# A gated delta-rule layer with a ternary feed-forward: softmax and key scales of the projection cut into five pieces, and two scale vectors loaded in another stage

## What is computed

```python
q, k, v = (silu(causal_conv4(x @ W.T)) for W in (Wq, Wk, Wv))     # 4 heads of 64
beta    = sigmoid(x @ Wb.T)
delta   = chunked delta rule over 32 tokens (l2norm(q), l2norm(k), v*beta)
probs   = softmax((x @ gate_w + gate_b) / exp(log_temp), over 5)
probs   = probs * (1 - 5*eps) + eps
o       = probs[0..2] * (fir3(v), fir15(v), fir63(v)) + probs[3]*delta + probs[4]*v
x       = layernorm(x + rmsnorm(o) @ Wo.T)
```

## Time and profile before

| | us |
|---|---|
| median of 3 runs (2244.39 to 2247.52) | 2244.57 |
| the profiled execution's own time | 2240.09 |
| its span, first to last instruction | 2238.3 |
| PE busy in the span | 2050.4 (92%) |
| DVE / ACT / POOL busy | 1161.4 / 875.1 / 535.1 |

### The profile page before, as it was taken

One profiled execution on the slowest core, in us unless ns is written; L12 is line 12 of the kernel. 1 busy time (PEld: TensorE's weight loads), 2 busy tenths in 40 slices (PEclk: granted clock), 3 DMA queues, 4 the chain that ended last, 5 costly groups with the idle time before them and its releaser, 6 DMA issues.

```text
span 2238.3 us, 42120 instructions
## 1 busy us (share of the span) xinstructions
PE 2050.4 (92%) x17462; PEld 1741.1 (78%) x17462; DVE 1161.4 (52%) x1836; ACT 875.1 (39%) x1418; POOL 535.1 (24%) x628
## 2 busy tenths in 40 slices
PE   6887876875899999799999999999999999999998
PEld 5766665775888887588888888888888888888886
DVE  5878786885467676424434434433443443443442
ACT  4444443102344444334434433443443443443442
POOL 1237872885455555000000000000000000000000
PEclk9989997987799999899999999999999999999999
DMA  6655555987999996100000000000000000000000
GB/s 180 192 155 167 175 159 164 299 260 227 199 220 242 228 229 171 37 1 29 1 29 29 6 23 29 29 1 29 29 1 29 29 1 29 29 1 29 29 1 19
DMA packets 250623, 208.81 MB, mean 93 GB/s; under 512 B 159634, under 2 KB 215378, under 8 KB 247890
## 3 DMA queue, kind: packets, MB, share of 16 engines
q1 hardware_dynamic: 238162, 175.84, 29.0%
q10 hardware_dynamic: 12288, 30.41, 4.8%
HBM read 126.32 MB, written 75.76 MB: 90 GB/s over the span
## 4 chain that ended last, share of the span: by engine, by line
PE 57%; issue 1%; DVE 1%; ACT 1%; DMA 0%; ACTq 0%; POOLq 0%; DVEq 0%; SPq 0%; POOL 0%
PE B L1622 50%; PE O L1649 5%; PE T L1580 1%; DVE yb L1755 0%; ACT gate L1694 0%; DMA srow<-in_srow 0%; DVE stats L1817 0%; ACT L1694 0%; DVE z L1808 0%; DVE z L1812 0%; DVE xl L1735 0%; DVE z L1831 0%; POOLq L1522 0%; ACT xh L1682 0%; ACTq L1516 0%
## 5 line engine op out<-in xcount | busy, mean ns | idle before, releaser
L1708 ACT ACTIVATE yb<-B,scol 128x512 f32<-128x512 f32 x256 | 176.6, 690 | 580.3 <-PE B L1622 580.3
L1622 PE MATMUL B<-act1l,wr 128*128 128x512 f32 x1024 | 398.4, 389 | 0.0
L1622 PE MATMUL B<-act0h,wr 128*128 128x512 f32 x1024 | 398.3, 389 | 0.0
L1622 PE MATMUL B<-act0l,wr 128*128 128x512 f32 x1024 | 398.3, 389 | 0.0
L1622 PE MATMUL B<-act1h,wr 128*128 128x512 f32 x1024 | 398.3, 389 | 0.0
L1743 DVE TENSOR_TENSOR act0l<-yb,act0h 128x512 fp32r<-128x512 f32 x256 | 176.1, 688 | 317.3 <-ACT act0h L1711 315.1
L295 PE MATMUL proj<-xt,w_qkv 128*128 128x262 f32 x768 | 203.4, 414 | 74.8 <-DVE acc L466 61.6
L466 DVE SCALAR_TENSOR_TENSOR acc<-proj,taps,acc 128x512 f32<-128x512 f32 x288 | 213.9, 749 | 82.6 <-ACT acc L413 74.4
L1743 DVE TENSOR_TENSOR act1l<-yb,act1h 128x512 fp32r<-128x512 f32 x128 | 88.6, 692 | 295.5 <-ACT act1h L1711 295.5
L295 PEld LDWEIGHTS proj<-xt,w_qkv 128*128 128x128 f32 x768 | 147.5, 201 | 116.8 <-DVE acc L466 69.8
L1622 PEld LDWEIGHTS B<-act1l,wr 128*128 128x128 f32 x1024 | 192.2, 188 | 39.9
(11 more groups left out here) (177 smaller groups left out, 3174.3 us busy)
## 6 DMA issues: line engine op xcount, KB each, us to landing
qk_s<-yT SPq DMA_DIRECT2D x16, 1024.0 KB, 5.1
qk<-qk_s SPq DMA_DIRECT2D x32, 512.0 KB, 4.7
wraw<-in_ffn_w ACTq DMA_DIRECT2D x32, 352.0 KB, 4.9
toe<-in_toe_short ACTq DMA_DIRECT2D x32, 320.0 KB, 7.4
xt<-in_xt SPq DMA_DIRECT2D x16, 524.0 KB, 4.2
toe<-in_toe_long ACTq DMA_DIRECT2D x32, 256.0 KB, 6.0
kk_s<-kfull SPq DMA_DIRECT2D x16, 512.0 KB, 5.1
k_s<-ktok SPq DMA_DIRECT2D x16, 512.0 KB, 6.0
```

Source lines behind the costliest of these rows:

```text
L1622: last = nc.tensor.matmul(B[slot % 4][:, :], w, part, start=(k == 0 and i == 0), stop=(k == kts - 1 and i == len(parts) - 1))
L1708: last = nc.scalar.activation(dst, B[slot % 4][:, :], ACT.Gelu, scale=scol[:, slot:slot + 1])
```

## The change

In project the boundary work is cut into five pieces, put between the blocks of three steps t = 4c + 5, 4c + 6 and 4c + 7, which is 5, 6, 7 for part 0, 9, 10, 11 for part 1 and 13, 14, 15 for part 2: logits behind block 1 and maxima (with ssk0) behind block 2 of the first; key scales behind block 5 of the second; sums behind block 1 and shares behind block 2 of the third. Both exponentials go on ACT ahead of the tap of block 3 in the second step. The turning of the key scales and their copies move from the first to the third step, and POOL's substitution starts and ends one step later. The loads of `scol` and `srow` move from the head of ffn to the end of delta, behind those of `x1` and `xres`, with their tiles and their semaphore; the waits stay. The helpers `gate_logits` and `gate_shares` are cut in two, and part 3 calls them one after the other as before.

```diff
--- before.py
+++ after.py
-EARLY_COLS = {6: (0, 1, 8), 7: (0, 8, 14), 8: (0, 14, 20), 9: (0, 20, 31),
-              10: (1, 1, 8), 11: (1, 8, 14), 12: (1, 14, 20), 13: (1, 20, 27), 14: (1, 27, 31)}
+EARLY_COLS = {7: (0, 1, 8), 8: (0, 8, 14), 9: (0, 14, 20), 10: (0, 20, 31),
+              11: (1, 1, 8), 12: (1, 8, 14), 13: (1, 14, 20), 14: (1, 20, 26), 15: (1, 26, 31)}
...
-                    if c in range(EARLY) and t % PART_STEPS == 0:
+                    if c in range(EARLY) and t % PART_STEPS == 2:
...
+                def exponentials(t):
+
+                    c = t // PART_STEPS - 1
+                    if c in range(PARTS - 1) and t % PART_STEPS == 2:
+                        act.wait_ge(to_exp0, c + 1)
+                        if c < EARLY:
+                            act.wait_ge(small_out, (c + 1) * PART_STEPS + 1)
+                            if c:
+                                act.wait_ge(gam0_done, c)
+                            nc.scalar.activation(ebeta[:, :, :], raw[:, c * NE:c * NE + NE, NGATE:NGATE + HEADS], ACT.Exp,
+                                                 scale=-1.0).then_inc(exp0_done, 1)
+                        nc.scalar.activation(lg0[:, :, :, :], lg0[:, :, :, :], ACT.Exp).then_inc(exp0_done, 1)
...
                     for cb in range(CB):
+                        if cb == 3:
+                            exponentials(t)
...
                     step(t, t % 2, (t - 1) // 2, True, t < 2)
-                    if t % PART_STEPS == 0:
-                        c = t // PART_STEPS - 1
-                        act.wait_ge(small_out, t + 1)
-                        if c < EARLY:
-                            if c:
-                                act.wait_ge(gam0_done, c)
-                            nc.scalar.activation(ebeta[:, :, :], raw[:, c * NE:c * NE + NE, NGATE:NGATE + HEADS], ACT.Exp,
-                                                 scale=-1.0).then_inc(exp0_done, 1)
-                        act.wait_ge(to_exp0, c + 1)
-                        nc.scalar.activation(lg0[:, :, :, :], lg0[:, :, :, :], ACT.Exp).then_inc(exp0_done, 1)
...
-                    gate_logits(nc, link, keep, lg0, mx0, rows(c)).then_inc(to_exp0, 1)
-
-                def first_shares(c):
-                    dve.wait_ge(exp0_done, c + 1 + min(c + 1, EARLY))
-                    link(gate_shares(nc, link, keep, lg0, mx0, rows(c)))
+                    gate_logits(nc, link, keep, lg0, rows(c))
+
+                def first_maxima(c):
+                    gate_maxima(nc, link, lg0, mx0).then_inc(to_exp0, 1)
+                    if c < EARLY:
+                        dve.wait_ge(kk_summed, (c + 1) * PART_STEPS + 2)
+                        nc.vector.tensor_scalar(ssk0[:, :, :].rearrange("p (t b) h -> p t (b h)", b=BATCH),
+                                                kk[:, c * PART_STEPS:(c + 1) * PART_STEPS, :], L2_EPS, None, ALU.add)
 
                 def first_scales(c):
 
-                    dve.wait_ge(kk_summed, (c + 1) * PART_STEPS + 2)
-                    nc.vector.tensor_scalar(ssk0[:, :, :].rearrange("p (t b) h -> p t (b h)", b=BATCH),
-                                            kk[:, c * PART_STEPS:(c + 1) * PART_STEPS, :], L2_EPS, None, ALU.add)
                     dve.wait_ge(exp0_done, 2 * c + 1)
...
+                def first_sums(c):
+                    dve.wait_ge(exp0_done, c + 1 + min(c + 1, EARLY))
+                    gate_sums(nc, link, keep, lg0, mx0, rows(c))
+
+                def first_shares(c):
+                    link(gate_shares(nc, link, keep, lg0, mx0, rows(c)))
+
                 def step(t, p, n, follow):
+
+                    c = (t - 1) // PART_STEPS - 1
+                    at = (t - 1) % PART_STEPS if c >= 0 else None
                     for cb in range(CB):
                         convolution(t, cb)
+                        if at == 0 and cb == 1:
+                            first_logits(c)
+                        if at == 0 and cb == 2:
+                            first_maxima(c)
+                        if at == 1 and cb == CB - 1 and c < EARLY:
+                            first_scales(c)
+                        if at == 2 and cb == 1:
+                            first_sums(c)
+                        if at == 2 and cb == 2:
+                            first_shares(c)
                         if follow and cb == 2:
                             small_copies(t - 1)
...
                     step(t, t % 2, (t - 1) // 2, True)
-                    if t % PART_STEPS == 0:
-                        first_logits(t // PART_STEPS - 1)
-                        if t // PART_STEPS <= EARLY:
-                            first_scales(t // PART_STEPS - 1)
-                    if t % PART_STEPS == 1 and t > 1:
-                        first_shares(t // PART_STEPS - 1)
...
+                sp.dma_start(keep["scol"][:, :], io["scol"]).then_inc(keep["par_in"], 16)
+                src = io["srow"]
+                sp.dma_start(keep["srow"][:, :], bass.AP(tensor=src.tensor, offset=0, ap=[[0, P], [1, D]])).then_inc(keep["par_in"], 16)
...
-                sp.dma_start(scol[:, :], io["scol"]).then_inc(par_in, 16)
-                src = io["srow"]
-                sp.dma_start(srow[:, :], bass.AP(tensor=src.tensor, offset=0, ap=[[0, P], [1, D]])).then_inc(par_in, 16)
                 load(1, 1)
```

More of the change, by code:

```diff
@@ L599, in early_rows, with gate_logits @@
     sub.scaled_rows().then_inc(keep["inv_done"][0], 1)
-def gate_logits(nc, link, keep, lg, mx, rows):
+def gate_logits(nc, link, keep, lg, rows):
     temp = bcast(bcast_mid(keep["itemp"][:, :], rows.stop - rows.start), 5)
@@ L607, in gate_logits, with gate_maxima @@
     link(nc.vector.tensor_tensor(lg[:, :, :, :], lg[:, :, :, :], temp, ALU.mult))
+def gate_maxima(nc, link, lg, mx):
     lgf = lg[:, :, :, :].rearrange("p t h f -> p (t h) f")
@@ L610, in gate_logits, with gate_sums @@
     return nc.vector.tensor_tensor(lgf, lgf, bcast(mx[:, :], 5), ALU.subtract)
-def gate_shares(nc, link, keep, lg, mx, rows):
+def gate_sums(nc, link, keep, lg, mx, rows):
     n = rows.stop - rows.start
@@ L620, in gate_shares @@
     link(nc.vector.tensor_tensor(by_head, by_head, bcast_mid(keep["slope"][:, :], n), ALU.mult))
+def gate_shares(nc, link, keep, lg, mx, rows):
+    n = rows.stop - rows.start
+    lgf = lg[:, :, :, :].rearrange("p t h f -> p (t h) f")
     link(nc.vector.tensor_tensor(lgf, lgf, bcast(mx[:, :], 5), ALU.mult))
@@ L842, in link @@
                     dve.wait_ge(chain, links[0])
-                gate_logits(nc, link, keep, lg, mx, LAST).then_inc(to_exp, 1)
+                gate_logits(nc, link, keep, lg, LAST)
+                gate_maxima(nc, link, lg, mx).then_inc(to_exp, 1)
                 link(nc.vector.tensor_scalar(ssk[:, :, :].rearrange("p (t b) h -> p t (b h)", b=BATCH), kk[:, :, :],
@@ L853, in _ @@
                 dve.wait_ge(exps, 2)
+                gate_sums(nc, link, keep, lg, mx, LAST)
                 gate_shares(nc, link, keep, lg, mx, LAST).then_inc(pw_done, 1)
@@ L1469, in ffn @@
     with outer.ctx:
-        scol = outer.sb("scol", [P, 4 * HT])
-        srow = outer.sb("srow", [P, D])
+        scol, srow = keep["scol"], keep["srow"]
         power = outer.sb("power5", [P, BATCH])
@@ L1498, in ffn @@
             full = [slow.sb(f"full{i}", [P, HT, TOK]) for i in range(2)]
-        par_in, power_set = outer.sem("p5_par_in"), outer.sem("p5_power_set")
+        par_in, power_set = keep["par_in"], outer.sem("p5_power_set")
         x_in, out_stored, w_in = keep["x1_in"], outer.pair("p5_out_stored"), outer.pair("p5_w_in")
@@ L1926, in build @@
                     ("stats1", 6), ("mv1", 2), ("rstd1", 1)))
-                keep["x1_in"] = late.pair("p5_x_in")
+                keep["scol"], keep["srow"] = late.sb("scol", [P, 4 * HT]), late.sb("srow", [P, D])
+                keep["x1_in"], keep["par_in"] = late.pair("p5_x_in"), late.sem("p5_par_in")
                 for n in ("xres_in", "x1_sum", "st1_done", "var1_done", "rs1_link", "rstd1_done", "x1_ready"):
```

## The result

| | before | after |
|---|---|---|
| median of the compared runs, us | 2246.05 (4 runs, 2244.39 to 2252.86) | 2224.09 (4 runs, 2222.82 to 2225.38) |
| ratio | | 0.9897, interval 0.9874 to 0.9919 |
| profiled execution, us (span) | 2240.09 (2238.3) | 2222.82 (2221.0) |

The change made the kernel faster, by 22 us in the medians and 17.3 us between the two profiled executions (what follows explains the 17.3). The forecast was 2229 in a range of 2213 to 2236.

What follows compares the result with a forecast made beforehand. Waits, not a full engine, bound the projection and the feed-forward's head. Excess 30.7 less 20.5 saves 10.2, with A 14.7: 2225.4 from the profiled 2240.1; the median stands 4.5 above, 2229.9; forecast 2229, range 2213 to 2236.

Steps and rivals of the forecast that it cites:

- A: Head of the feed-forward: moving the loads of scol and srow earlier saves 4.5 us, bounds 3.7 to 5.1.
- B: Projection: pieces put between blocks cut the steps' excess from 30.7 to 20.5 us, saving 10.2 us.
- Late next is the turned tile at 912.72: Feed-forward's head: without the load wait, ACT's split waits only for PE's turned tile, starting about 912.75 instead of 917.30.
- all behind it moves rigidly: Feed-forward's head: everything behind ACT's split comes earlier by the same 4.5 us.
- the squares don't hold DVE: Rival, projection: first and third steps keep 1.74 us of cover each; B saves 26, total 2214; 15 in 100.
- The lateness of POOL in step 11: POOL's columns 20 to 30 end about 10.7 us into step 11, delaying the shares; block 3 starts 5.0 us late.
- part 1's 10.25: New excess of steps 9 to 11: 3.0 first, 0.25 and 1.0 second, 5.0 third, 1.0 clock.
- the 1.0 for the clock: Step 11: 1.0 us added for a low clock, as PE's wait for block 5 grows to 5.5 us.
- The excess before: Projection: time of the steps around the parts' ends beyond ordinary 19.55 us steps, 30.7 us in all.
- the clock rival: PE's longer wait for block 5 brings low-clock stretches in six first and third steps; 10 us slower, 2254; 3 in 100.
- the loads weren't what held ACT: Rival, feed-forward's head: the flag's read is slow while loads are under way; only B gains, 2234; 7 in 100.
- the change doesn't do what it says: Rival: a late key square makes line 485 wait in step 11, costing up to 5 us, 2234; 5 in 100.

## Why the prediction was right, and where it was not

- **Sign and size.** 22 us against a forecast of 15.6 (from 2244.6), and 17.3 against 14.7 in the profiled pair. The total is nearer than its parts, and that is luck: A gave 3.6 us less than forecast and B, in this pair, 4.3 more (0.9 + 14.5 = 15.4 against 14.7), and 5.8 us came from a stage I had left out, with 1.9 and 2.0 lost again in the first steps and the convolutions.
- **Part A, the failed step.** "Late next is the turned tile at 912.72": it is late next for ACT, as the split at 1.98 us behind the turning shows, but "all behind it moves rigidly" is wrong. PE's own flag read and branch follow its turning and take to 901.73. The row was there to be seen: PE goes through the same branch as ACT. 4.5 forecast, 1.5 at the head, 0.9 in the stage. With the branch swapped the head gains 4.55.
- **Part B, mechanism.** POOL's squares hold the subtraction and the shares. Rival "the squares don't hold DVE" is refuted by line 632 (1.66 us, ending 0.36 behind sqk), by the kernel without the squares and by the one with the pieces away from them. The lateness of POOL in step 11 came as described: line 162 ended at 249.81, 11.0 us into the step (predicted 10.7), and the second product behind sq.
- **Part B, sizes.** All large terms were somewhat too big: part 1's 10.25 measured 8.0. Its second step took 0.62, not 1.25 (of the three scale pieces that meet POOL the reciprocal, 0.55 us, wasn't held). Step 11 took 4.84, not 6.0: block 3 starts 252.75 - 238.81 = 13.9 us into it (predicted 14.1), and all of the excess is that; the 1.0 for the clock should have been nothing. In step 15 no column of POOL came between (3.2 predicted, 2.3 at block 3, 1.9 in the end): line 648 went ahead of the square. Second steps were 0.30 for 0.25.
- **The excess before was taken as fixed.** 30.7 holds 5.3 us of a low stretch that the same code doesn't always show. The pieces save 14.5 us where it falls and 25.8 - 16.2 = 9.6 where it doesn't; the 10.2 forecast lies between only because its own terms were too large. With the clock rival I had asked whether new low stretches would fall in the pieces' new places. The clock does fall in four of them (0.92 in steps 7, 9 and 13, 0.86 in step 11), but it cost nothing there: block 3's lateness alone, 2.3, 2.6, 1.7 and 4.8 us, is their whole excess.
- **Queues.** SP's two issues, the turning and the copies in step 7, and the key square (line 485's wait) cost nothing to be seen. The rival "the loads weren't what held ACT" fell with the chain; "the change doesn't do what it says" fell with step 11 at 24.39 us.

## What to carry to other kernels

When a wait at the head of a stage is taken away, list what every engine does there before its first real instruction, flag reads and branches too; try the body that runs directly behind the test (3 us at the head here, less or nothing in the whole stage). Before putting DVE work into a hole, look at what POOL runs in it: a product with two SBUF inputs waits out a POOL instruction that reads SBUF (1.66 us for 0.49 here), so the hole behind block 5 was worth more than the one behind block 2. And compare a kernel with itself before explaining a few us: here identical code gave 4.5.

## What was not expected of the hardware

- A branch over a long body left PE without work for 2.94 us, and for 0.04 when the running body came first.
- The granted clock's low stretches fall in some executions of the same code and not in others (step 5: 26.29 us at 0.74, 22.55 at 0.92); with the step behind it that is 5.3 us.
- With the feed-forward's tiles at other places a 128x512 matmul took 394 to 395 instead of 389 ns, most of 26 us in the stage. Whether by bank, by port or otherwise was not tried.
- DVE and POOL take turns: of two products in a row, one started 0.01 us ahead of the square and only the next waited; POOL's square beside them took 2.22 instead of 1.89 us.
